# One-hots of 128 places beside values in two sets of columns, and an earlier wait for the gate and up weights

## The reference, cut to what matters

```python
x = x + 0.5 * ffn(layernorm(x)); x = x + attention(layernorm(x)); x = x + 0.5 * ffn(layernorm(x))

def ffn(x):                                   # 4 batches, 8 experts, k = 1024 // 8 * 2 = 256
    affinity = softmax(x @ gate_w.T)          # per token over the experts
    gating, idx = top_k(affinity.T, 256)      # each expert takes its 256 best tokens of each batch
    x_in = x[b, idx]
    h = silu(x_in @ w_gate[e].T) * (x_in @ w_up[e].T)        # 128 -> 512
    out[b, idx] += gating * (h @ w_down[e].T)                # 512 -> 128
```

## Time and profile before

| | |
|---|---|
| median of 3 runs | 1235.25 us (1233.53 to 1240.15) |
| the profiled execution, its own time | 1234.61 us |
| span of its trace | 1232.8 us |
| PE busy | 1077.9 us, 87% |
| DVE busy | 981.6 us, 80% |
| ACT busy | 774.1 us, 63% |
| POOL busy | 581.3 us, 47% |
| granted PE clock, mean | 0.968 of full speed |
| moved by DMA | 93.84 MB, mean 76 GB/s |

### The profile page before, as it was taken

How to read it: one execution, slowest core, us unless ns; L and a number is a source line. 1 busy time by engine, 2 the same in 40 slices (tenths; PEclk the granted TensorE clock), 3 DMA queues, 4 the chain that set the end, 5 groups by cost and what they waited for, 6 DMA issues and landing times. The chain is left out here.

```text
span 1232.8 us, 25059 instructions
## 1 busy us (share of the span) xinstructions
PE 1077.9 (87%) x9344; PEld 460.9 (37%) x9344; DVE 981.6 (80%) x1938; ACT 774.1 (63%) x1466; POOL 581.3 (47%) x610
## 2 busy tenths in 40 slices
PE   3159899899499899999999999999998889899994
PEld 3036565566232122222222222222222247565653
DVE  3675976676879899999999999999997675976541
ACT  2035232523258899999989999899999835222220
POOL 3034878665546331010011466355621177678885
PEclk9999999899688899999999999999999989999997
DMA  8004455447803131211021121111310125345452
GB/s 261 31 25 112 89 102 126 101 87 184 206 35 96 30 92 42 58 42 44 24 57 41 42 61 34 48 42 41 95 44 5 26 78 118 82 92 118 93 117 24
DMA packets 93056, 93.84 MB, mean 76 GB/s; under 512 B 14668, under 2 KB 70220, under 8 KB 92904
## 3 DMA queue, kind: packets, MB, share of 16 engines
q1 hardware_dynamic: 70408, 75.46, 21.9%
q0 software_dynamic: 22528, 16.79, 9.9%
HBM read 64.02 MB, written 30.13 MB: 76 GB/s over the span
## 5 line engine op out<-in xcount | busy, mean ns | idle before, releaser
L1785 DVE TENSOR_REDUCE mx<-pA 128x2 f32<-128x1024 f32 x512 | 585.8, 1217 | 18.3 <-PE pA L1344 17.8
L1105 ACT ACTIVATE Pt<-pS 128x512 f32<-128x512 f32 x1024 | 556.3, 596 | 33.9 <-PE pS L1429 28.5
L1408 PE MATMUL pO<-Pt,Vst 128*16 128x256 f32 x4096 | 323.0, 387 | 13.4 <-ACT U L1096 12.8
L1004 ACT ACTIVATE Pt<-pS 128x512 f32<-128x512 f32 x128 | 76.3, 596 | 212.8 <-PE pS L1273 180.4
L614 POOL DMA_INDIRECT xg<-zd,idx x128 | 126.4, 987 | 164.1 <-DVE idx L1592 92.2
L1344 PE MATMUL pA<-Kst,Qst 48*128 48x512 bf16 x704 | 140.6, 396 | 20.4 <-DVE mx L1785 19.1
L1273 PE MATMUL pS<-Pt,wg 128*128 128x512 f32 x256 | 140.0, 630 | 12.5 <-issue 9.8
L1408 PEld LDWEIGHTS pO<-Pt,Vst 128*16 128x16 f32 x4096 | 68.2, 94 | 206.9 <-issue 109.8
L1429 PE MATMUL pS<-Qst,Kst 51*128 51x512 bf16 x704 | 138.6, 390 | 7.1 <-ACT Pt L1105 4.1
L685 POOL TENSOR_TENSOR mparts<-mx,onesm 128x32 bf16<-128x32 f32 x16 | 4.0, 252 | 262.1 <-DVE mx L1790 205.9
L1284 PEld LDWEIGHTS pA<-wd,Pt 128*128 128x128 f32 x960 | 114.3, 193 | 17.1 <-issue 16.5
(11 more groups left out here) (214 smaller groups left out, 1160.4 us busy)
## 6 DMA issues: line engine op xcount, KB each, us to landing
wg<-w_gate_dram SPq DMA_DIRECT2D x32, 256.0 KB
wu<-w_up_dram SPq DMA_DIRECT2D x32, 256.0 KB
wd<-w_down_dram SPq DMA_DIRECT2D x32, 256.0 KB
qk<-parts SPq DMA_DIRECT2D x64, 96.0 KB
Kst<-qk SPq DMA_DIRECT2D x132, 32.0 KB
zd<-Z SPq DMA_DIRECT2D x8, 512.0 KB
vp<-pair SPq DMA_DIRECT2D x4, 1024.0 KB
Vst<-vp SPq DMA_DIRECT2D x16, 256.0 KB
```

The source lines that it names most:

```text
L1105: S.activation(Pt[:, s % 4, j, r * 512:(r + 1) * 512], pS[:, bank_of(k, 4 * s + 2 * j + r), :], ACT.Exp, scale=SCALE).then_inc(s_exp, 1)
L1408: last = M.matmul(pO[32 * h:32 * h + 16, cols], Vst[k][:, s % 8, h, :], Pt[:, s % 4, h // 2, (h % 2) * 512 + 256 * a:(h % 2) * 512 + 256 * ...
L1785: V.reduce_max(mx2[:, k, 2 * j:2 * j + 2, c, half], pA[ring[q, a] % 2][:, :, :], AX.X).then_inc(s_Ar, 1)
```

## The change

`onehots` compares only with the places 0 to 127 and writes 128 columns. So that a place of 128 to 255 is not lost, each token's values now stand in one of two sets of five columns: set 1 if its place is 128 or more, else set 0, with zeros in the other. A one-hot chunk is then multiplied once with ten columns: 16 products for each expert in place of 32. Two places are compared as one: `place_in` is the place less 128 where `upper` is 1.

`upper` and `place_in` are two more DVE instructions at the end of each of the four selections, with a wait each. `by_slot(hh)` fills the two sets: a product `vals * upper` and a difference, of 640 elements a partition each. It stands on POOL for hh = 0 (ahead of `gather(0)`) and hh = 2 (ahead of `gather(16)`), on DVE for hh = 1 (after `all_onehots(8)`) and hh = 3 (after `all_onehots(24)`). `compact` waits for `s_columns` where it waited for `s_vals`.

`load_weights(j)` issues the gate and up weights after `s_up >= 4 * (j - 1)`, which is the last up product of expert j - 2, and only the down weights after `s_down >= j - 1`.

`room`, which shared its memory with `onehot` in attention, keeps its size; `onehot` is now its first half.

```diff
             def load_weights(j):
+                e, p = j % E, j % 2
+                if j >= 2:
+                    sp.wait_ge(s_up, 4 * (j - 1))
+                sp.dma_start(wg[p][:, :], t["w_gate"][e]).then_inc(s_w[p], 16)
+                sp.dma_start(wu[p][:, :], t["w_up"][e]).then_inc(s_w[p], 16)
                 if j >= 2:
                     sp.wait_ge(s_down, j - 1)
-                e, p = j % E, j % 2
-                sp.dma_start(wg[p][:, :], t["w_gate"][e]).then_inc(s_w[p], 16)
-                sp.dma_start(wu[p][:, :], t["w_up"][e]).then_inc(s_w[p], 16)
                 sp.dma_start(wd[p][:, :, :], ...).then_inc(s_w[p], 16)
...
+            def by_slot(hh):                                   # on POOL; the same on DVE
+                v = vals[hh % 2][:, :, :, :]
+                high = upper[hh % 2][:, :, :].unsqueeze(3).to_broadcast([P, HT, E, 5])
+                to = columns[hh % 2]
+                pool.wait_ge(s_vals, 6 * hh + 6)
+                pool.wait_ge(s_upper, hh + 1)
+                GP.tensor_tensor(to[:, :, :, 1, :], v, high, ALU.mult).then_inc(s_above, 1)
+                pool.wait_ge(s_above, hh + 1)
+                GP.tensor_tensor(to[:, :, :, 0, :], v, to[:, :, :, 1, :], ALU.subtract).then_inc(s_columns, 1)
...
             pool.wait_ge(s_fill, 2)
             gains(0)
+            by_slot(0)
             gather(0)
             gather(1)
...
+            by_slot(2)
             gather(RUN)
             gather(RUN + 1)
...
                 if j % E == 0:
-                    pe.wait_ge(s_vals, 6 * (j // E + 1))
+                    pe.wait_ge(s_columns, j // E + 1)
                 for b in range(HB):
                     pe.wait_ge(s_onehot, 2 * j + b + 1)
-                    for s in range(SH):
-                        for c in range(CH):
-                            last = M.matmul(pI[:, (b * SH + s) * 5:(b * SH + s + 1) * 5],
-                                            onehot[:, b, c, s * P:(s + 1) * P], vals[j // E % 2][:, c * HB + b, j % E, :],
-                                            start=(c == 0), stop=(c == CH - 1))
+                    for c in range(CH):
+                        last = M.matmul(pI[:, b * SH * 5:(b + 1) * SH * 5], onehot[:, b, c, :],
+                                        columns[j // E % 2][:, c * HB + b, j % E, :, :].rearrange("p s f -> p (s f)"),
+                                        start=(c == 0), stop=(c == CH - 1))
...
-                    V.tensor_scalar(slotT[hh % 2]..., bank[:, 0:P], -1.0, None, ALU.add).then_inc(signal_read(key), 1)
+                    V.tensor_scalar(flat(upper[hh % 2]), bank[:, 0:P], float(P + 1), None, ALU.is_ge).then_inc(s_upper, 1)
+                    V.tensor_scalar(flat(slotT), bank[:, 0:P], -1.0, None, ALU.add).then_inc(signal_read(key), 1)
+                    dve.wait_ge(s_upper, hh + 1)
                     dve.wait_ge(*was_read(key))
+                    link(V.scalar_tensor_tensor(flat(place_in[hh % 2]), flat(upper[hh % 2]), -float(P), flat(slotT),
+                                                ALU.mult, ALU.add))
...
-                    last = V.tensor_scalar(onehot[:, b, c, :], slots[:, :], slotT[j // E % 2][:, c * HB + b, e:e + 1], None,
-                                           ALU.is_equal)
+                    last = V.tensor_scalar(onehot[:, b, c, :], slots[:, 0:P], place_in[j // E % 2][:, c * HB + b, e:e + 1], None,
+                                           ALU.is_equal)
...
                 if (it, k) == (6, 0):
                     all_onehots(8)
+                    by_slot(1)
...
                 if (it, k) == (22, 1):
                     all_onehots(24)
+                    by_slot(3)
```

More of the change, by code:

```diff
@@ L163, in program @@
         slotp = sb("slotp", [P, P], BF16)
-        slotT = [sb(f"slotT{h}", [P, HT, E], F32) for h in range(2)]
+        slotT = sb("slotT", [P, HT, E], F32)
+        upper = [sb(f"upper{h}", [P, HT, E], BF16) for h in range(2)]
+        place_in = [sb(f"place_in{h}", [P, HT, E], F32) for h in range(2)]
+        columns = [sb(f"columns{h}", [P, HT, E, SH, 5], BF16) for h in range(2)]
         vals = [sb(f"vals{h}", [P, HT, E, 5], BF16) for h in range(2)]
@@ L168, in program @@
         res = [sb(f"res{i}", [P, CH, ROWS_H], F32) for i in range(2)]
-        onehot = sb("onehot", [P, HB, CH, CAP], BF16)
+        room = sb("room", [P, 2, N], F32)
+        onehot = room[:, 0, :].bitcast(BF16).rearrange("p (b c s) -> p b c s", b=HB, c=CH)
         row = sb("row", [P, HB * SH], F32)
@@ L212, in program @@
         num, den = scr[:, 0:2, :], scr[:, 2:4, :]
-        room = onehot[:, :, :, :].rearrange("p b c s -> p (b c s)").bitcast(F32).rearrange("p (i n) -> p i n", i=2)
         pairs = {4: (scr[:, 0, :], scr[:, 2, :]), 5: (scr[:, 1, :], scr[:, 3, :]), 6: (room[:, 0, :], room[:, 1, :]),
@@ L269, in program @@
         s_onehot = sem("onehot")
+        s_upper = sem("upper")
+        s_above = sem("above")
+        s_columns = sem("columns")
         s_comp = sem("comp")
@@ L1552, in front @@
                 else:
-                    V.tensor_scalar(slotT[hh % 2][:, :, :].rearrange("p t e -> p (t e)"), bank[:, 0:P], -1.0, None,
-                                    ALU.add).then_inc(signal_read(key), 1)
+                    flat = lambda a: a[:, :, :].rearrange("p t e -> p (t e)")
+                    V.tensor_scalar(flat(upper[hh % 2]), bank[:, 0:P], float(P + 1), None, ALU.is_ge).then_inc(s_upper, 1)
+                    V.tensor_scalar(flat(slotT), bank[:, 0:P], -1.0, None, ALU.add).then_inc(signal_read(key), 1)
+                    dve.wait_ge(s_upper, hh + 1)
                     dve.wait_ge(*was_read(key))
+                    link(V.scalar_tensor_tensor(flat(place_in[hh % 2]), flat(upper[hh % 2]), -float(P), flat(slotT),
+                                                ALU.mult, ALU.add))
             def affinities(hh):
@@ L1572, in affinities, with by_slot @@
                 last.then_inc(s_affc, 1)
+            def by_slot(hh):
+                v = vals[hh % 2][:, :, :, :]
+                high = upper[hh % 2][:, :, :].unsqueeze(3).to_broadcast([P, HT, E, 5])
+                to = columns[hh % 2]
+                dve.wait_ge(s_vals, 6 * hh + 6)
+                V.tensor_tensor(to[:, :, :, 1, :], v, high, ALU.mult).then_inc(s_above, 1)
+                dve.wait_ge(s_above, hh + 1)
+                V.tensor_tensor(to[:, :, :, 0, :], v, to[:, :, :, 1, :], ALU.subtract).then_inc(s_columns, 1)
             def onehots(j, quarter):
```

## The result

The changed kernel took 1230.7 us in the median of 10 runs (1226.69 to 1234.45), the kernel before, run beside it, 1237.98 (1233.53 to 1243.61). The ratio is 0.9946 with a 95% interval of 0.9927 to 0.9965: faster by 7.3 us. The forecast was 1224.5, a gain of 10.6. Three later measurements of the unaltered kernel, on three chips, gave 0.9993 (0.9976 to 1.001), 0.9960 (0.9942 to 0.9978) and 0.9980 (0.9962 to 0.9998): 2.0, 5.1 and 2.4 us. So the sign was right, though the interval of 0.9993 includes no change; the forecast gain was 1.5 times the first measurement and 2 to 5 times the later ones.

The account below looks back on a forecast made before the run. No engine was taken to bound all stages: DVE bounds attention and selection, PE the expert windows, with POOL full too. Terms -4.4 - 0.5 - 0.6 - 5.1 = -10.6 gave a forecast of 1224.5 us, range 1220 to 1228, widened by rivals to 1216 and 1231.

Parts of the forecast that it names:

- what PE waited for: Gate products of late experts and expert 10 wait for weights still in transfer; earlier loads remove 4.7 and 1.97 us.
- R4: Rival: PE waits for turned tokens or a buffer, not weights, so those waits stay; 1228 us, chance 0.12.
- the cap: From gather(25) on POOL is full; PE could gain 8.9 us, but only POOL's 5.10 us idle before scatter(30) is saved.
- The sign of being wrong: Forecast is wrong if expert stretches in 1104 to 1198 us get shorter than POOL's 12.5 us for an expert.
- R1: Rival: POOL holds nothing back, so 0.7 us in expert 10 and a few at the end come on top; about 1218, chance 0.16.
- R3: Rival: slower, as each indirect transfer on full POOL takes longer beside the weights; at 0.2 us each 1247, chance 0.08.
- the instructions: Per expert, compact saves 0.39 us and one-hots 35 ns each; a column pair takes 3.1 us on POOL, 1.65 on DVE.
- R2: Rival: columns are dear, by_slot costing 6 us a pair on POOL and 3.3 on DVE; 1231 us, chance 0.16.
- At its end, in expert 22, nothing covers anything ... +1.7: End of last selection: two DVE instructions 0.6, one-hots -0.55, by_slot(3) 1.65, and compact(24) waits for all: +1.7 us.
- Experts 0 to 5 ... Together -1.9: Compact saves 0.39 us each in experts 0 and 2, shorter one-hots 1.1 in 3 to 5: -1.9 us.
- The first stage: From the start through experts 11 to 13: 2.3 - 1.9 - 0.4 - 3.2 - 1.2 = -4.4 us.
- from there to gather(16): End of attention: two compacts save 0.8 us, but compact waits 0.3 for POOL's pair and the one-hots; net -0.5.

Follow-up runs that it names:

- before_fill: The kernel before with idle PE filled by products ident x ident before gate product 2 and in experts 11 and 16: 1231.16 us, 0.9981 of the kernel before.
- first_columns: The changed kernel with columns filled on DVE in two parts, the first expert's ahead of its one-hots: 1223.45 us, 0.993 of the kernel before.
- weights_alone: The kernel before with only the new load_weights, the earlier wait for gate and up weights: 1232.37 us, 0.9983 of the kernel before.
- onehots_alone: The changed kernel with the old load_weights, so one wait for all three weights: 1235.65 us, 1.0025 of the kernel before.
- after_fill_again: Second run of the changed kernel with 8, 14, 11 and 14 products ident x ident in four PE waits: 1226.48 us, 0.9938 of the kernel before.

## Why the prediction was right, and where it failed

*Right: what PE waited for.* Late weights; the waits of the earlier trace rows went or shrank, the one of 2.11 us went, and POOL's idle time before scatter(30) with them. R4 fell. The wait of 1.97 us before expert 10 is no such proof: it is gone (0.05 us) in `before_fill` too, with the old loads.

*Right: the cap.* The end brought 4.7 to 4.8 us in all four profiles where 5.1 was forecast, neither more nor less, though PE could have gained more. From gather(25) to gather(31) an expert takes 12.63 to 12.65 us in the four, and 12.64 in the kernel before: POOL's pace. (The sign of being wrong that I had set, an expert stretch shorter than POOL's 12.5, was badly put: by the gate products of 24 to 31 an expert takes 11.9 us in three of the four, as PE catches up with POOL, and the cap held.) Reading POOL's busy time together with its 0.30 us of issue gave that number, and R1 fell with it. R3 fell too: a gather's mean is 984 ns for 987, that of the three groups of scatters 1.57 to 1.62 us for 1.57 to 1.60.

*Right: the instructions.* One-hot 33 ns shorter (35), compact 0.38 us in the chain for 0.78, 0.40 less for an expert (0.39), DVE's pair of 640 elements 1.65 us (1.65). POOL's pair was 2.58 where I took 3.1: the line through f32 rows was too dear for bf16, hence +1.84 and not +2.3 at the start. R2 fell. On the start the Trainium skill, "SBUF — State Buffer", section "Who interferes with whom", was the rule that spoke against the placement, and the trace agrees: `place_in` takes 1.27 us beside POOL's instruction of 1.28, and 0.29 in `first_columns`, where POOL has none.

*Failed: "At its end, in expert 22, nothing covers anything ... +1.7".* The term counted what DVE adds, and that was exact: with the fill it measured 1.36 and 1.49. What it left out is what PE's idle time does: 3.6 us without a product, and a clock of 0.69 over 11 us, which delays the turn of 23's tokens; for that gather(25) waits, as its row says (2.57 us, released by L1284). From there POOL is full, so nothing makes the delay good. The term was +2.8 to +3.9 against the profile I forecast from; about 1 us of that is the profile's luck, as `before_fill` and `weights_alone` show (+0.96, +1.14 with no columns to wait for). I had used this effect where it was in my favour (1.5 us back at expert 31) and not where it was against me.

*Failed: "Experts 0 to 5 ... Together -1.9".* "load_weights(2) stands behind a store and gains nothing" is right, but its wait was taken as fixed. Product 2 waits 1.3 to 1.4 us longer, and after it the clock falls for 3.4 to 6.8 us. I had put this down to load 3; `onehots_alone` has the wait without it, so its cause is open. Product 4 stood at +1.8 to +6.0 after a start of +1.84. The first stage came to -0.6, -1.6, -4.6 and -2.5, mean -2.3, where -4.4 was forecast. Here, however, the size isn't settled. The profile of the kernel before shows a clock of 1.00 from 100 to 155 us; the same stretch in the kernel before filled, in the weights alone and in the kernel before with half scatters shows 0.97. So a fall of the clock there comes without the change too; one profiled execution had luck where the others had none, and I forecast from it.

*Failed: the range.* It held the first median, 1230.7, by 0.3 us. By gain it asked for 4 to 19 us, and two of four measurements are outside, with 2.0 and 2.4. All its cases moved work; only R2 names the clock, for attention, and none prices it, though in one kernel the executions go from 1227 us (at 0.966) to 1234 us (at 0.959). The rival that I should have written is "the new idle time is paid twice".

Still open: on the last chip the unfilled change was worth 2.4 us and the clock behind the filled waits, by the estimate above, 2.3 more; 5.9 of the 10.6 are missing even so. By the landmarks of `after_fill_again` they are missing in the first stage (-1.74 us at product 15, against -4.4) and from there to gather(16) (+1.41 against -0.5). In those two steps four executions of one kernel differ by 4 us and by 2.3. Which share is load 3, which the chance of where the clock falls and which a favourable execution of the kernel before, the runs don't tell.

## What to carry to other kernels

An instruction put into a place where nothing hides it costs its duration on the engine that waits, and, if that is PE, it can cost as much again as lower clock in what follows (here 1.4 to 2.4 us on top of 1.4); price both, and look for another part of the work to put first (an eighth of the columns was enough). Before an engine's saving is counted, add issue time to the busy time of every engine that queues small transfers: if that is full, the saving ends at that engine's next idle time. And forecast from landmarks of several executions, of the kernel before above all: here one step was reproducible to 0.2 us and its neighbour varied by 4, and the one profile that the forecast rested on had a clock of 1.00 in two places where others of nearly the same code had less.

## What the hardware showed that was not expected

Products that compute nothing, put into waits of PE, made the kernel 3.5 and 3.95 us faster, with a granted clock of 1.00 in place of 0.69 where the wait had been 3.6 us. A lower clock of 3.4 us also followed waits of only 0.6 and 1.0 us (`weights_alone`, 0.84 over 11 us), in some executions and not in others. An indirect scatter of half the rows took 1.42 to 1.48 us against 1.57 to 1.62. A POOL instruction of 640 bf16 elements a partition took 1.28 us, where 512 in f32 take 1.27. And `place_in`, which POOL's arithmetic stretched from 0.29 to 1.27 us, took 0.29 at 1090.99 in the changed kernel, in the middle of one of POOL's scatters (1090.71 to 1092.26).
